# Router gates of a mixture-of-experts kernel: gate weights held in the array in four column groups, a copy and a transpose back, and a changed order around them

## The reference, cut to what matters

```python
x = layernorm(x + attention(x))                       # x1 in the kernel
gate_out = einsum('bsd,ed->bse', x, Wg)               # 8 gates for each token, in full fp32
top_v, top_i = top_k(gate_out, 2)
probs = softmax(top_v)
for e in range(8):
    w_e = sum(probs * (top_i == e))
    h1, h2 = x @ W1[e].T, x @ W2[e].T
    out += ((h1 * sigmoid(h1) * h2) @ W3[e].T) * w_e
x = layernorm(x + out)
```

## Time and profile before

| | |
|---|---|
| time of the profiled execution | 1172.77 us |
| its span, first to last instruction | 1170.9 us |
| steps 0 to 15 | to about 462 us |
| experts | about 498 to 1115 us |
| mean granted TensorE clock | 0.963 of 2.4 GHz |
| TensorE matmuls busy | 1077.8 us |
| VectorE busy | 904.9 us |
| GpSimd busy | 658.1 us |
| ScalarE busy | 632.9 us |

### The profile page before, as it was taken

One profiled execution on the slowest core, in us unless ns is written; L12 is line 12 of the kernel. 1 busy time (PEld: TensorE's weight loads), 2 busy tenths in 40 slices (PEclk: granted clock), 3 DMA queues, 4 the chain that ended last, 5 costly groups with the idle time before them and its releaser, 6 DMA issues. The chain is left out here.

```text
span 1170.9 us, 22198 instructions
## 1 busy us (share of the span) xinstructions
PE 1077.8 (92%) x6674; PEld 957.9 (82%) x6674; DVE 904.9 (77%) x1990; ACT 632.9 (54%) x1085; POOL 658.1 (56%) x558
## 2 busy tenths in 40 slices
PE   6899999999999998798999999999999999999900
PEld 5678888888888887687888988888899999999900
DVE  5678888888888888666776677777777888888736
ACT  3445555555555553464445455656566666666528
POOL 1111554545454554574787677667757767677434
PEclk9899999999999999988999999999999999999955
DMA  4011222111121121656566787878778899989469
GB/s 180 19 43 66 55 55 54 56 54 54 54 54 54 54 55 37 163 123 186 113 131 162 167 198 202 205 184 219 192 192 212 238 257 237 240 239 239 93 208 384
DMA packets 81633, 167.72 MB, mean 143 GB/s; under 512 B 28224, under 2 KB 45504, under 8 KB 81312
## 3 DMA queue, kind: packets, MB, share of 16 engines
q1 hardware_dynamic: 51552, 131.39, 36.4%
q0 software_dynamic: 30016, 35.55, 16.7%
HBM read 121.79 MB, written 45.09 MB: 143 GB/s over the span
## 5 line engine op out<-in xcount | busy, mean ns | idle before, releaser
L867 POOL DMA_INDIRECT x_acc<-fy_sb,pair_out x135 | 252.0, 1867 | 119.7 <-DVE fy_sb L1133 42.6
L1404 PE MATMUL ring<-fxh,fw_hi 128*128 128x256 f32 (+1 forms) x720 | 236.5, 328 | 0.5 <-DVE gated L1107 0.4
L1406 PE MATMUL ring<-fxh,fw_lo 128*128 128x256 f32 (+1 forms) x720 | 234.6, 326 | 0.0
L1405 PE MATMUL ring<-fxl,fw_hi 128*128 128x256 f32 (+1 forms) x720 | 234.3, 325 | 0.0
L627 ACT ACTIVATE fw_hi<-w_raw 128x1024 fp32r<-128x1024 f32 x162 | 169.7, 1054 | 83.9 <-PE out L1471 81.6
L953 DVE TENSOR_TENSOR fw_lo<-w_raw,fw_hi 128x1024 fp32r<-128x1024 f32 x162 | 196.6, 1220 | 15.0 <-ACT fw_hi L627 14.8
L102 POOL DMA_INDIRECT xg<-x_src,pair_in x135 | 153.6, 1138 | 75.5 <-issue 50.0
L795 POOL TENSOR_TENSOR rs<-ve,neg_half 128x4 f32<-128x4 f32 x48 | 56.6, 1180 | 235.2 <-DVE nm L904 235.2
L92 POOL DMA_INDIRECT slot_list<-pairs,slot_u x128 | 136.5, 1067 | 46.7 <-issue 32.1
L1235 PE MATMUL ring<-xh,w_hi 128*128 128x512 f32 x384 | 158.6, 413 | 2.3 <-issue 2.1
L1469 PE MATMUL out<-fw_hi,gh 128*128 128x256 f32 x540 | 155.9, 289 | 0.0
(11 more groups left out here) (151 smaller groups left out, 2031.7 us busy)
## 6 DMA issues: line engine op xcount, KB each, us to landing
w_raw<-w_ffn SPq DMA_DIRECT2D x162, 512.0 KB, 5.1
x_in<-h SPq DMA_DIRECT2D x16, 512.0 KB, 3.3
x_src<-x SPq DMA_DIRECT2D x16, 512.0 KB, 4.3
x_acc<-x SPq DMA_DIRECT2D x16, 512.0 KB, 5.6
acc<-x_acc SPq DMA_DIRECT2D x16, 512.0 KB, 7.5
out<-o SPq DMA_DIRECT2D x16, 512.0 KB, 6.3
xg<-x_src,pair_in POOLq DMA_INDIRECT x135
x_acc<-fy_sb,pair_out POOLq DMA_INDIRECT x135
```

The lines of the kernel that those rows point to most:

```text
L867: nc.gpsimd.indirect_dma_start(x_acc, bass.IndirectOffsetOnAxis(pair_out[j][:, q, 0:1].bitcast(U32), 0), fy[j][:, q, :], None, compute_op= ...
L1404: nc.tensor.matmul(out, hi, rows_hi, start=dc == 0, stop=False)
L1405: nc.tensor.matmul(out, hi, rows_lo, start=False, stop=False)
L1406: last = nc.tensor.matmul(out, lo, rows_hi, start=False, stop=dc == DC - 1)
```

## The change

The gate weights are padded from 8 to 32 columns (zeros) on the host. `gates` now makes `wg` (32 columns) the stationary operand and `x1T` the moving one (128 tokens): the four token tiles go to the four groups of 32 array columns, that is to partitions 0, 32, 64 and 96 of `out1_0`. The result has gates on the partitions, so a new ScalarE step `keep_gates` copies 128x128 to `gate_cols`, and a new TensorE step `turn_gates` transposes it into the second half of `out1_0`, from where `choose` reads. The semaphore `gate_columns` is new, and `gate_columns_kept`; `gates` is now raised by `turn_gates`. And the order changes: on TensorE `gates` goes before the third product of half 0, `turn_gates` after it, and `transpose(0)` after the first two products of half 1. (In step 16 `turn_gates` stands behind all three products of half 0.) On VectorE `place` goes before `x_lo(0)`. In xstep 1 `rank_products` goes from behind unit 1 to behind unit 2, and `place` from behind the gate of unit 2 to behind that of unit 3.

```diff
+GATE = P // Q
...
-        wg = sb("wg", [P, DC, E])
+        wg = sb("wg", [P, DC, GATE])
+        gate_cols = sb("gate_cols", [P, P])
...
 def keep_x1T(s):
-                        act.wait_ge(s_g, s - 3)
+                        act.wait_ge(s_gc, s - 3)
...
+            def keep_gates(s):
+                act.wait_ge(s_gc, s - 2)
+                if within(s, 4, CHUNKS + 2):
+                    act.wait_ge(s_g, s - 3)
+                nc.scalar.activation(gate_cols[:, :], out1[0][:, 0, 0:P], ACT.Copy).then_inc(s_gk, 1)
...
 @block.scalar
...
             def step(s, half, j):
                     keep_x1T(s)
+                if within(s, 3, CHUNKS - 1):
+                    keep_gates(s)
                 if within(s, 1, CHUNKS - 2):
                     act.wait_ge(s_pt[0], s * 2 + 2)
                     normalize(0, x_in[:, 1 - j, :, :], normed[0], s + 1, s_n[0])
+                if at(s, CHUNKS):
+                    keep_gates(s)
...
             def xstep(s, half, j, spot):
+                if at(s, 0) or at(s, 1):
+                    keep_gates(CHUNKS + 1 + s)
...
 @block.vector
...
             def choose(m, j):
-                link(m, 1, nc.vector.tensor_copy(g[:, :, :], out1[0][:, 0, 0:Q * E].rearrange("p (q e) -> p q e", q=Q)))
+                link(m, 1, nc.vector.tensor_copy(g[:, :, :], out1[0][:, 1, 0:P].rearrange("p (q c) -> p q c", q=Q)[:, :, 0:E]))
...
             def step(s, half, j):
+                if within(s, 3, CHUNKS + 2):
+                    place(s - 3, half, j)
                 if within(s, 1, CHUNKS - 2):
                     x_lo(0, s + 1)
-                if within(s, 3, CHUNKS + 2):
-                    place(s - 3, half, j)
...
             def xstep(s, half, j, spot):
-                    if at(s, 1) and u == 2:
+                    if at(s, 1) and u == 3:
                         place(CHUNKS - 1, CHUNKS // 2 + 1, 0)
...
 @block.tensor
...
             def gates(s, last_user, count):
-                for q in range(Q):
-                    for dc in range(DC):
-                        last = nc.tensor.matmul(out1[0][:, 0, q * E:(q + 1) * E], x1T[:, dc, q * P:(q + 1) * P],
-                                                wg[:, dc, :], start=dc == 0, stop=dc == DC - 1)
-                last.then_inc(s_g, 1)
+                for dc in range(DC):
+                    for q in range(Q):
+                        last = nc.tensor.matmul(out1[0][q * GATE:(q + 1) * GATE, 0, 0:P], wg[:, dc, :],
+                                                x1T[:, dc, q * P:(q + 1) * P], start=dc == 0, stop=dc == DC - 1)
+                last.then_inc(s_gc, 1)
+
+            def turn_gates(s):
+                pe.wait_ge(s_gk, s - 2)
+                nc.tensor.transpose(out1[0][:, 1, 0:P], gate_cols[:, :], ident[:, :]).then_inc(s_g, 1)
...
             def step(s, half, j):
-                        project(1, s, s - 1, 0, j)
+                        project(1, s, s - 1, 0, j, (0, 1))
                     if within(s, 3, CHUNKS):
                         gates(s, s_res, s * 2)
+                    if layer2:
+                        project(1, s, s - 1, 0, j, (2,))
+                    if within(s, 3, CHUNKS):
+                        turn_gates(s)
+                if layer2:
+                    project(1, s, s - 1, 1, j, (0, 1))
                 if within(s, 1, CHUNKS - 2):
                     pe.wait_ge(s_n[0], s + 2)
...
                     transpose(0, s + 1, normed[0])
-                if layer2:
-                    project(1, s, s - 1, 1, j, (0, 1))
...
             def xstep(s, half, j, spot):
                         hidden(s, j, u, spot)
+                        if at(s, 0) and u == 0:
+                            turn_gates(CHUNKS + 1)
...
-                        if at(s, 1) and u == 1:
+                        if at(s, 1) and u == 0:
+                            turn_gates(CHUNKS + 2)
+                        if at(s, 1) and u == 2:
                             rank_products(CHUNKS + 2)
```

More of the change, by code:

```diff
@@ L330, in attention_and_experts @@
         s_st = [sem("x1_stored0"), sem("x1_stored1")]
+        s_gc, s_gk = sem("gate_columns"), sem("gate_columns_kept")
         s_x1T, s_g, s_rt, s_gap, s_prob = sem("x1T_ready"), sem("gates"), sem("router_steps"), sem("gap_ready"), sem("probs_ready")
@@ L1654 @@
         "ln_wb": np.ascontiguousarray(wb),
-        "w_gate": by_partition(np.asarray(L0_ffn_Wg).T, D),
+        "w_gate": np.pad(by_partition(np.asarray(L0_ffn_Wg).T, D), ((0, 0), (0, 0), (0, GATE - E))),
         "w_ffn": np.ascontiguousarray(np.concatenate([w1, w2, w3], axis=1)),
```

## The result

The median of four runs is 1154.01 us (1153.4 to 1156.74), where four runs of the kernel before gave 1170.55 us (1168.64 to 1172.96). The ratio is 0.9859 [0.9842, 0.9876]: faster by 1.4%, some 16.5 us. I had forecast 1161.5, and a range of 1155.5 to 1172.0. The profiled execution took 1154.48 us (before 1172.77), its span 1152.6.

A forecast was written before the change was run, and what follows sets the result against it. The prediction took a loop between TensorE and VectorE to bound each router step; 13 steps at -4.6 us and xstep 1 at -3.7 gave -8.3, from a median of 1169.83 to 1161.5 us, range 1155.5 to 1172.

The forecast's parts named there:

- The loop it rested on: Router steps: `rows3` to the gates' end, VectorE from `choose` to the next `xl`, for which TensorE waits.
- The limit: Router steps: VectorE's own work ahead of `choose`, ending at 252.41, limits the gain to 0.78 us a step.
- X: Time of the 16 gate records in the new shape, with going in and a reserve: put at 1.17 us.
- likeliest case: Gates: 16 records in the time of 9, X = 1.17; step changes by -0.35 us; 1161.5 us, chance 0.48.
- rival 3: Gates: all four groups at once, X = 0.61, -0.91 a step held at -0.78; 1156.0 us, chance 0.14.
- bounds of 0.61 and 1.88: Gates' time X: four groups wholly at once, 0.61 us; all 16 records one behind another, 1.88 us.
- my own sum: Router step, `rows3` to VectorE's start of `choose`: 6.90 us before, 5.38 + X after, so X - 1.52 a step.
- Rival 1: Gates: groups run serially, shape changes empty the array, 0.16 each; X = 2.20, +0.68 a step, 1174.9 us, chance 0.14.
- Beside the gates: Router steps: copy 0.3 us, turn hidden behind the third product, `k_sb` wait 0 to 0.2 us costed at nothing.
- Xstep 1: First experts: wait for `picked` shrinks to about 1.3 us, clock stays 2.4 GHz, gain 3.7 us; 2 if it falls.
- The second wait: Xstep 1: TensorE waits about 1.5 us for `slot_u` ahead of the y products.
- Step 16: `choose` waits for three more products: at most 1 us later, inside TensorE's 3.84 us wait for gathered rows.

The follow-up runs named there:

- order-only kernel: The changed kernel's new order with the old gates (x1T stationary, 8 moving columns, no copy, no turn): 1158.82 us, 0.9891 to the kernel before.
- the second set in four groups: The changed kernel with a second set of the same 16 gate records ahead of the first, in the same four column groups: 1161.12 us, 0.9917.
- the other two traces: Two repeats of the unchanged changed kernel, each profiled again: 1156.90 us (0.9868) and 1155.19 us (0.9854).
- the better kernel: The changed kernel with GpSimd's rstd of chunk 15 ahead of its eight scatters: 1152.63 us (0.9842), and again 1152.19 us (0.9837).
- the kernel with the second set in group 0: The changed kernel with a second set of 16 narrow records ahead of the gates, all in one column group: 1176.50 us, 1.0047.

## Why the prediction was wrong

**The loop it rested on** was right. A step was bound by the way from `rows3` to `g`, and the gain came as VectorE's idle time ahead of `choose`. The limit was not: I had put it at 0.78 us, at the end of `nm`. In the order-only kernel `g` starts 0.07 us after the start of `nm`, where it was 0.93 before, so the room was 0.86. The piece fell by 0.73 and the period by 0.81, past the 0.78 that I had named as a sign of being wrong; where the other 0.08 comes from wasn't followed up.

**The step that failed is X, the time of the gates:** put at 1.17 us, measured 0.58. The likeliest case assumed that the two records of one matmul follow each other and that only the first of the next group runs beside the second of this one, 16 records in the time of 9. In the trace all four groups run at once, 16 records in the time of four (0.46), with about 0.1 more until the next product starts (246.34 - 245.79 = 0.55 for the second set in four groups, against 0.46 for the first). That is rival 3, which had X = 0.61 and a chance of 0.14. I took 1.17 as the case that "asks for the least from the hardware"; but between bounds of 0.61 and 1.88 the cautious middle was no mechanism with a row behind it, and nothing made it more likely than the end where separate groups don't hinder one another. The issue order, on which I hung the argument, made no difference (0.60 against 0.58). With X = 0.58 my own sum gives 5.38 + 0.58 - 6.90 = -0.94 a step, held at -0.78: over twelve periods -9.4, measured -9.7. That they agree is in part luck: the rest of the piece, put at 5.38, measured 6.17 - 0.58 = 5.59, and the limit was 0.08 too low. The Trainium skill, page "TensorE: Matmul & The Clock Gate", section "Measured speedup vs the span model", counts about 4 ns for each further tile of a pack; here the trace agrees in kind, 6 to 7 ns between the starts of the four records of a round. Its 2.38x for three column tiles is 0.79 a tile, and I had carried it over to four tiles as 0.8 us. The sets in one group and in four show 1.77/0.46 = 3.8x here, 0.96 a tile.

**Rival 1** fell with the groups running at once, but a wait of the size of its drain is in the trace. The last record of the gates and the last transpose ahead of a product in the kernel before:

```profile
244.84 0.27 PE L1295 MATMUL out<-x1T,wg 128*32 128x128 f32 x1
```

```profile
253.80 0.27 PE L1193 MATMUL tp<-ident,normed 128*128 128x128 f32 x1
```

Behind fp32 work at full width the product starts 253.83 - 253.80 = 0.03 us later, behind the narrow gates 245.04 - 244.84 = 0.20. Going into the narrow shape took 244.46 - 244.15 = 0.31, going into `output(0)` at full width 258.36 - 258.13 = 0.23. That is 0.17 and some 0.08 more than the same switches at full width, 0.25 together, where rival 1 had 0.16 each and I had 0.08 as a reserve. The first of the two lies inside X. The Trainium skill, page "TensorEngine Tiling (Array Packing)", section "Key Properties", says that a change of tiling mode drains the engine; the trace is in keeping with that, but no run sets a drain apart from other causes.

**Beside the gates** the costs were as worked out. The copy took 0.28 us (0.3), it ran while the third product did, and the turn didn't wait for it in steps 3 to 15. `k_sb` ended at 247.32 + 0.67 = 247.99 and the product that needs its bank started at 248.05; in the whole kernel TensorE waited 1.5 us for `k_sb`. The transposes behind two products, which I had at nothing, gained 0.7 us in step 2 by the trace.

**Xstep 1** was right for the moves by themselves: -3.7 forecast, -3.8 alone, with the clock at 1.00. On top of the new gates it wasn't sure to come. From unit 0 of xstep 1 to the y products the gain is 4.6 us in the first trace, and 1.7 and 2.0 in the other two, where the clock fell in unit 3; I had given 2 for that case. The second wait is 1.14 us (1.5). The gates' change in xsteps -1 and 0 gave nothing, as forecast, but for another reason than the one given. At unit 0 of xstep 0 the changed kernel is 14.4 us ahead (488.11 against 502.54), 2.3 more than at `g` of step 15; at unit 0 of xstep 1 it is 12.5 ahead (507.65 against 520.13). The 2 us went at the wait of 2.70 us for `x`, with the half clock behind it. In the other two traces the lead at unit 0 of xstep 1 is 12.6 and 12.9, and 12.6 and 12.4 at `g` of step 15, so nothing gained either; the wait for `x` is the same and the clock behind it 1.00. I hadn't looked at GpSimd's queue there, and had named only `fxl`.

**Step 16** was costed at up to 1 us inside a cover. TensorE's row in the changed kernel:

```profile
472.10 0.33 PE L1302 MATMUL out<-ident,gate_cols 128*128 128x128 f32 x1 [2.54 <-ACT gate_cols L609]
```

The copy is queued behind ScalarE's other normalization, so the turn waits 2.54 us and `g` comes at 472.46. The cover held: TensorE's wait for gathered rows is 1.42 us where it was 3.84, and 2.53 and 2.71 in the other two traces. So it shrank by 1.1 to 2.4 us, where I had at most 1.

**The sum.** Forecast -8.3; measured -18.3 of span. Of the 10 us of miss the 13 router steps make 5.5 (0.4 + 9.7 measured, 4.6 forecast), the start 1.3, step 2 0.7, the first experts 1.3 (5.0 measured, 3.7 forecast), and the rest up to the end 1.2. The last two aren't shown to be effects of the change. The first experts gave 5.0 in this trace and 1.6 and 2.5 in the other two of the same kernel, and behind the y products of xstep 1 the kernels here have 629.1 to 634.0 us. By the medians the miss is 8.2 us, of which the steps and the start are 7.5. The range failed with it: its lower end, 1155.5, was nearly the time of rival 3 alone, 1156.0, with nothing below it for small terms of the same sign.

## What to carry to other kernels

- When an operation has never run in a kernel, its rows give only ends. Take each end as a mechanism and ask what in the rows speaks for it; a value between them that "asks for the least" is a mixture, not a case. Let the range go past the best case by the small terms that were costed at nothing.
- In a loop through several engines, a shorter operation counts only with the order behind it: the same gates cost 0.42 us a step when the turn stood behind eight transposes, and brought the step to within some 0.1 us of VectorE's own work when the copy and the turn were ready in time. Cost the time until the last consumer, engine queue by engine queue.
- After a gain upstream, look for the next queue that was just in time: here GpSimd's `rstd` between scatters left a wait of 2.7 us, and moving it ahead gave 3 us. And profile the same kernel more than once before a stretch behind such waits is priced: its parts moved by up to 3.5 us between three traces, while the loop's repeated within 0.02.

## What the runs showed of the hardware

- Groups of 32 array columns run beside one another in whichever of the two orders the program issues them: four records every 0.109 us with 128 moving columns, 0.056 with 64 and 0.216 with 256, by their single starts. Within one group they follow one another, 0.109 apart.
- Going into these narrow records from full-width fp32r work took 0.31 us where the same switch at full width took 0.23, and coming out 0.20 where it took 0.03.
- The granted clock behind a wait differed between executions of one kernel. Behind the 2.70 us for `x` it was 0.50 in one trace of the changed kernel and 1.00 in another (2.79 us and 1.00 in the third); behind 2.09 and 2.19 us for `picked` it fell to 0.50, and behind 2.38 us in the better kernel it stayed at 1.00.
- Starts in the trace aren't in the program's order across groups: in the kernel with the second set in group 0, three records of later matmuls start at 253.50, ahead of the last of that set at 253.60. The records don't name their group; I take them for groups that had nothing ahead of them.
- Making the narrow operand (8, padded to 32 columns) stationary and the 128 tokens moving, in four column groups, took 16 records from 1.70 to 0.58 us, though the products that count are the same. The groups did it, not the swap: in one group such records take 1.77 us.
